# Expert stage of a two-layer graph network: new order on TensorE, rings of six instead of four, two reload rules instead of one, tile numbers read eight at a time

## The reference, cut to what matters

```python
xf = x.reshape(-1, D)                         # 6250 x 256, layer-normed
idx = jnp.argmax(xf @ router_w.T + router_b, axis=-1)
h = jnp.einsum('nd,ndh->nh', xf, jnp.take(W1, idx, axis=0)) + jnp.take(b1, idx, axis=0)
h = jax.nn.relu(h)                            # 64 hidden features
out = jnp.einsum('nh,nhd->nd', h, jnp.take(W2, idx, axis=0)) + jnp.take(b2, idx, axis=0)
out = jax.nn.relu(out)
```

## Time and profile before

| what | value |
|---|---|
| median of three executions | 3842.12 us |
| the profiled execution's own time | 3842.25 us |
| its span, first to last instruction | 3840.7 us |
| TensorE busy | 2751.5 us (72% of the span) |
| GpSimd busy | 2512.2 us (65%) |
| VectorE busy | 1879.0 us (49%) |
| ScalarE busy | 796.1 us (21%) |
| mean granted TensorE clock | 0.905 |

### The profile page before, as it was taken

One profiled execution on the slowest core, in us unless ns is written; L12 is line 12 of the kernel. 1 busy time (PEld: TensorE's weight loads), 2 busy tenths in 40 slices (PEclk: granted clock), 3 DMA queues, 4 the chain that ended last, 5 costly groups with the idle time before them and its releaser, 6 DMA issues. The chain is left out here.

```text
span 3840.7 us, 42526 instructions
## 1 busy us (share of the span) xinstructions
PE 2751.5 (72%) x12338; PEld 2079.1 (54%) x12338; DVE 1879.0 (49%) x5797; ACT 796.1 (21%) x1977; POOL 2512.2 (65%) x2689
## 2 busy tenths in 40 slices
PE   3787777777777658667777777665667767777769
PEld 2565555565544545555655555543455555555547
DVE  6555457777626822633333333332455555555533
ACT  1111111111113313411111111110133333333320
POOL 5777777777730532667777777776777777777701
PEclk9999889989888879889889999887899999999969
DMA  5444435445432467844434444433344444444415
GB/s 163 117 123 123 129 112 144 140 140 144 125 94 95 155 182 205 243 136 135 136 114 125 126 125 122 115 111 96 108 124 125 122 123 125 125 122 125 125 39 186
DMA packets 279543, 501.74 MB, mean 131 GB/s; under 512 B 59771, under 2 KB 179969, under 8 KB 279162
## 3 DMA queue, kind: packets, MB, share of 16 engines
q0 software_dynamic: 126240, 345.85, 31.5%
q1 hardware_dynamic: 135916, 139.10, 11.8%
q10 hardware_dynamic: 17136, 13.84, 1.1%
HBM read 419.12 MB, written 79.18 MB: 130 GB/s over the span
## 5 line engine op out<-in xcount | busy, mean ns | idle before, releaser
L1473 PE MATMUL bank<-g,m 128*128 128x256 f32 (+1 forms) x4704 | 1447.3, 432 | 820.3 <-DMA g<-d_t,src_i 574.2
L1401 POOL DMA_INDIRECT g<-d_t,src_i x1568 | 1499.3, 956 | 510.2 <-issue 500.1
L1473 PEld LDWEIGHTS bank<-g,m 128*128 128x128 f32 x4704 | 874.3, 209 | 1117.8 <-issue 362.6
L1401 POOL DMA_INDIRECT g<-d_xn,src_i x784 | 761.2, 971 | 244.7 <-issue 235.5
L1426 DVE TENSOR_SCALAR m<-iota,rel_f,ew_f 128x128 f32<-128x128 f32 x2352 | 704.6, 364 | 263.2 <-PE bank L1473 258.1
L1437 DVE TENSOR_TENSOR accT<-bank,accT 128x256 f32 x294 | 122.7, 417 | 577.0 <-PE bank L1461 576.7
L1407 ACT ACTIVATE s<-bank 128x256 f32<-128x256 f32 (+1 forms) x294 | 111.6, 380 | 1050.7 <-PE bank L1475 540.2
L1425 DVE TENSOR_SCALAR eq<-iota,rel_f 128x128 bf16<-128x128 f32 x784 | 232.9, 297 | 140.6 <-PE bank L1475 140.6
L1475 PE MATMUL bank<-ones_b,eq 128*128 128x1 bf16 x784 | 135.5, 173 | 0.0
L219 POOL TENSOR_TENSOR rsd<-ved,mhalf 128x2 f32<-128x2 f32 (+1 forms) x25 | 18.9, 756 | 175.6 <-DVE ved L213 175.4
L174 POOL DMA_DIRECT2D out<-y x25 | 17.8, 714 | 165.4 <-DVE y L2585 165.4
(11 more groups left out here) (386 smaller groups left out, 4112.3 us busy)
## 6 DMA issues: line engine op xcount, KB each, us to landing
g<-d_t,src_i POOLq DMA_INDIRECT x1568, 2.8
side_xn<-d_xn SPq DMA_DIRECT2D x96, 256.0 KB, 3.2
g<-d_xn,src_i POOLq DMA_INDIRECT x784, 2.8
d_swT<-wkv SPq DMA_DIRECT2D x48, 256.0 KB, 3.0
swT<-d_swT SPq DMA_DIRECT2D x24, 512.0 KB, 3.7
xt<-d_xs POOLq DMA_DIRECT2D x80, 128.0 KB, 3.2
d_ys<-y ACTq DMA_DIRECT2D x80, 128.0 KB, 2.7
x<-in_x SPq DMA_DIRECT2D x24, 256.0 KB, 2.9
```

What stands on the lines that cost most here:

```text
L1401: pool.indirect_dma_start(g[n % RING][:, u, 0:D], None, table, bass.IndirectOffsetOnAxis(ap=k.src_i[:, t:t + 1], axis=0)).then_inc(gathere ...
L1473: ins = pe.matmul(b[:, 0:GW], m[o][:, u, :], g[r][:, u, :], start=(u == 0), stop=(u == GT - 1 and not count))
```

## The change

TensorE's order becomes inner, transpose, output. The rings become six deep. SyncE's one step becomes two: `load_in` reloads `w1` when the relu of the tile six before is done, and `load_out`, one tile behind and ahead of `load_in` in the order, reloads `w2` when the output product of the tile six before is done. GpSimd and SyncE read their tables eight numbers at a time, in one call each, when the first of the eight is needed and ahead of that tile's wait.

```diff
-    DEEP = 4
+    DEEP, AHEAD = 6, 8
...
+        def uses(j):
+            return (SORTED - j + DEEP - 1) // DEEP
+
+        def numbers(engine, table, top):
+            values = []
+
+            def of(t):
+                if t == len(values):
+                    values.extend(nc.values_load_multi_w_load_instructions(table[0:1, t:min(t + AHEAD, SORTED)], engines=[engine], min_val=0, max_val=top)[1])
+                return values[t]
+            return of
...
             def _(pool):
+                page = numbers(mybir.EngineType.Pool, k.tile_page, EXPERTS * REGION - 1)
                 def load(t):
                     r = t % DEEP
+                    x = page(t)
                     tails.landed(pool, t)
                     wait(pool, turned, t - DEEP + 1)
-                    x = pool.value_load(k.tile_page[0:1, t:t + 1], min_val=0, max_val=EXPERTS * REGION - 1)
...
             def _(sp):
                 sp.wait_ge(padded, 2 * DEEP)
-                def load(t):
-                    r = t % DEEP
+                expert = numbers(mybir.EngineType.SP, k.tile_expert, EXPERTS - 1)
+
+                def load_in(t):
+                    r, e = t % DEEP, expert(t)
+                    wait(sp, h_done, t - DEEP + 1)
+                    sp.dma_start(w1[r][:, 0:H2 + 1], a["expert_in"][bass.ds(e, 1), :, :].rearrange("a p h -> p (a h)")).then_inc(w_loaded[r], 16)
+
+                def load_out(t):
+                    r, e = t % DEEP, expert(t)
                     wait(sp, out_psum, t - DEEP + 1)
-                    e = sp.value_load(k.tile_expert[0:1, t:t + 1], min_val=0, max_val=EXPERTS - 1)
-                    sp.dma_start(w1[r][:, 0:H2 + 1], a["expert_in"][bass.ds(e, 1), :, :].rearrange("a p h -> p (a h)")).then_inc(w_loaded[r], 16)
                     sp.dma_start(w2[r][0:HID + 1, :], a["expert_out"][bass.ds(e, 1), :, :].rearrange("a h d -> h (a d)")).then_inc(v_loaded[r], 16)
-                tiles(sp, (load, 0))
+                tiles(sp, (load_out, 1), (load_in, 0))
...
-                tiles(pe, (turn, 0), (output, 2), (inner, 1))
+                tiles(pe, (inner, 1), (turn, 0), (output, 2))
```

More of the change, by code:

```diff
@@ L2204, in _ @@
                 for j in range(DEEP):
-                    pool.wait_ge(x_loaded[j], 16 * (SORTED // DEEP))
+                    pool.wait_ge(x_loaded[j], 16 * uses(j))
             @block.sync
@@ L2292, in _ @@
                 for j in range(DEEP):
-                    act.wait_ge(sent[j], 16 * (SORTED // DEEP))
+                    act.wait_ge(sent[j], 16 * uses(j))
 def stage_second_front(nc, kit, a, d):
```

## The result

The changed kernel takes 3812.48 us (median of four runs, 3810.81 to 3813.12) against 3843.26 us for the kernel before in its four runs (3837.87 to 3852.39). The ratio is 0.9914, with a 95% interval of 0.9902 to 0.9925: 31 us faster, where 22 were forecast. The profiled execution took 3810.81 us, with a span of 3809.3 us.

The account below looks back on a forecast made before the run. SyncE's issue time was taken as the bound, falling from 1.87 to 1.63 us a tile; the hand-over 24.7 us earlier, less 2.7 for slow reads, gave -22 us on 3842.25, so 3820 us, range 3802 to 3840.

Parts of the forecast that it names:

- Its issue time is the pace: SyncE in `stage_experts`: hardly waits, so its own 1.87 us per tile, plus the waits, paces the kernel before.
- the flat read: Rival: one load of eight costs 0.476 us, TensorE and DMA engines become the bound; 36 us gain, 3806 us; chance 0.23.
- the sum behind it: SyncE's stretch, 79 x 1.10 + 9 x 4.2 = 124.7 us: hand-over 24.7 us earlier, less 2.7 for slow reads and issues.
- the load of eight: SyncE's batched read of eight numbers: taken as 2.2 us, between 0.476 (one ordinary load) and 3.8 (eight of them).
- 1384.4 + 79 x 1.45 + 8.4: The flat read's hand-over to the next stage: first `w1` issue, 79 tile steps, then last `w1` to hand-over; 1507.4 us.
- none of it changes: Stage end: landing, products, store and barriers from the last `w1` to the hand-over stay at 8.4 us.
- at nothing: TensorE's new order: costed at no gain, hidden by the weights' issue, since the old 1.60 us loop keeps pace with SyncE's 1.63.
- the cover: SyncE's weight issue being slower than TensorE, hiding the order's effect; without it the order is worth up to 0.2 us a tile.
- Rings: Six-deep weight rings on SyncE: its 7.4 us of waits should hardly remain; 8.4 us long, enough to bridge most of a batch.
- The transfers: DMA time in the flat read: 0.69 x 161 / 80 = 1.39 us a tile, tying with PE's 1.38 us.

Follow-up runs that it names:

- the deepest run: Changed kernel with TensorE's order transpose, inner, output, no bounds checks, rings of eight and sixteen numbers to a batch; ratio 0.9855 to the kernel before.

## Why the prediction was right, and what in it was wrong

**Right: what bounds the kernel before.** "Its issue time is the pace", read from SyncE's cadence and its few waits. Order alone, rings alone and both together gain nothing; the batches alone gain 9 us and are the condition for the rest. Where the time came from is the one queue that the page's busy table doesn't list.

**Wrong: what bounds it after.** The forecast named its own sign of being wrong, "if the reads take under 1 us (then PE's loop must show near 1.4 us, and the DMA share above 0.9)". The reads took 0.782 us, the loop shows 1.46, and the share is 0.88 in the middle of the stage. So the mechanism is the flat read's, which had a chance of 0.23. The time, 3812 us, lies in the range because the range took in that rival; that 3820 comes within 8 us of it is in part luck, since the sum behind it has no loop of TensorE in it and a batch that is 1.3 us too long.

**The term that was mis-sized: the load of eight.** I took "8 x 0.271 = 2.2 us" between bounds of 0.476 and 3.8. It took 0.782, near the lower end: the single load's 0.476 is nearly all a price per instruction, and a further number costs (0.782 - 0.476)/7 = 0.044 us. The Trainium skill ("Runtime: NRT & Kernel Launch", "Instruction fetch mechanics") has about 0.2 us a register even in bulk; that is stated of HBM, and for this table in SBUF the trace doesn't agree. The checks came to (2.90 - 0.78)/8 = 0.26 us a number, 0.25 forecast, and the two loads of a tile to 1.04 us, 1.10 forecast. So the batch was 2.90 us instead of 4.2, SyncE's own time 1.40 us a tile instead of 1.63, and the forecast that it would keep the pace by itself did not come true.

**What took its place** is the case of the flat read: TensorE's loop as the bound, with SyncE level beside it. I gave that 36 us, and 31 came. The loop was put at 1.38 us and is 1.46: an inner product whose weights are loaded only after a wait is followed by the transpose after 0.54 us, not 0.44. But the sum went by 1.45 us a tile, so that is not where it fell short. Of its 1384.4 + 79 x 1.45 + 8.4 the start held (1384.8). The steps of `w1` came to 1.50 us, 4 us more in all. And the 8.4 us from the last `w1` to the hand-over became 1515.03 - 1503.3 = 11.7 us, because TensorE was by then behind SyncE: its last inner product began 1509.31 - 1503.3 = 6.0 us after that `w1`, before 1538.49 - 1535.51 = 3.0; "none of it changes" held only while SyncE was the pace. So the hand-over moved by 28.9 us and not by 36.5.

TensorE had fallen behind at two places. At the start it waited 2.5 us for the first weights, and the clock had yet to rise, as the changed kernel's first stretches show (columns as above; 0.50 and 0.72 are the granted clock):

```profile
1380.00:1390.00 10.00, 2.30 (x8) 1.57 (x8) 2.97 (x13) 0.36 (x1) 4.31 (x8) 0.50 0.48 133
1390.00:1400.00 10.00, 9.65 (x45) 7.71 (x46) 2.12 (x5) 3.73 (x10) 2.60 (x5) 0.72 0.66 182
```

And VectorE's two index instructions of 1.78 us (for tiles 40 and 42) hold up the copies in the loop: three steps there are 2.43, 1.90 and 2.02 us, 2.0 us more than 1.46 each.

**TensorE's order "at nothing".** Right for a SyncE of 1.63 us; at the 1.40 it has, the order is worth some 7 us. I had named up to 0.2 us a tile if the cover went: it is 1.60 - 1.46 = 0.14.

**Rings: the part read wrongest.** I priced them by SyncE's waits of before, 7.4 us, which were not even lost time, as the run with the rings alone shows. In the changed kernel six instead of four are worth the whole 31 us, in the old order 24 - 13 = 11 us. The waits of before say at most what a ring costs at the old pace. What it is worth after the change is set by the longest gap that it has to bridge, here a batch and a landing of 3.6 us; and I worked that gap out for six, but never for four.

**The transfers.** The 1.39 us a tile of DMA time, worked out from a share of 0.69, were used as a floor in the flat rival. The share doesn't scale so: by 0.69 at 197 GB/s, 330 GB/s would be a share of 1.16, and the deepest run shows 1.04. At 385.5 KB a tile 330 GB/s make 1.20 us.

## What to carry to other kernels

Read the queue that no busy table shows: a sequencer that never waits is a bound, and its own cadence against the engine's best step says how far a change can go. A batch of register reads trades many small delays for a few long ones, so size the rings for the longest gap, not for the mean rate, and expect the ring to decide whether the rest of the change pays. When an edit does nothing, try it together with the one against the limit beside it: two limits at the same height each hide the other.

## What the runs showed of the hardware that I had not expected

One register load from SBUF on SyncE took 0.476 us for one number, 0.782 for eight and 1.427 for sixteen (medians of 80, 10 and 5 loads): cheap to eight, 0.08 us a number from there on. A bounds check costs more than the number that it checks, 0.26 us against 0.04. And a stall of about two microseconds on TensorE, once in eight tiles, went in the run with rings of four with a mean granted clock of 0.85, while the same loop without the stalls, in the changed kernel, kept 1.00 in the same 80 us.
